# Neighbour sums in a graph network: one-hots compared with a row of numbers in PSUM and written tile by tile

## The chip, the cores and the metric

The kernel runs on one core of a Trainium2 chip, in one launch. Its time is the device time of that launch in microseconds (us); three runs are shown, with their median. A core has TensorE (PE, matrix products, with a separate row PEld for the loading of weights), VectorE (DVE), ScalarE (ACT), GpSimd (POOL) and SyncE (SP). SBUF is the working memory of 128 partitions, PSUM the smaller memory of eight banks into which TensorE writes.

## The reference

A graph of 12500 nodes with 32 features and 200000 edges, sorted by their target node, passes through four layers. The change touches the first only, a graph convolution that is applied three times:

```python
def _gcn_conv(x, src, dst, norm, W, b, n_nodes):
    h = x @ W
    msg = h[src] * norm[:, None]
    out = jax.ops.segment_sum(msg, dst, num_segments=n_nodes)
    return out + b
h = jax.nn.relu(_gcn_conv(x, src, dst, norm, W1, b1, n))
h = jax.nn.relu(_gcn_conv(h, src, dst, norm, W2, b2, n))
h = jax.nn.relu(_gcn_conv(h, src, dst, norm, W3, b3, n))
```

`norm` is a factor by node on each side, so what has to be summed for a node are rows of a table at `src`. After this layer come an attention over the same edges, a relational layer with edge types and a tensor product with edge attributes. Each gathers rows by edge and sums them by target node too.

## The kernel before, in words

The program is a row of blocks, one after the other; a barrier of all engines stands between two blocks. After the edges are sorted and tables are made, the three neighbour sums follow (`first_sums`, `second_sums`, `third_sums`; their tiles are called `sum0g`, `sum1g`, `sum2g` in the profile), then attention (`pass`), relational layer (`rel`) and tensor product (`sh`).

A neighbour sum takes the 200000 edges in 98 groups (`NG`) of 16 tiles of 128 edges (`GT` = 16). The rows to be summed are kept in device memory as three 16-bit parts whose sum is the 32-bit value. Five queues work on it:

- GpSimd issues one indirect DMA per tile of 128 edges (`_gather_groups`, L1241): 98 times 16, so 1568 gathers per sum. They write into a ring with four slots, one group each. Before a group it waits until its slot is free (L1237 to L1241, the semaphore `released`).
- SyncE passes on that a group has landed and that a slot is free (`_pass_groups`, L1244 and on; L1252 is where its word "landed" goes out).
- ScalarE copies the landed rows out of the ring (`copy_rows`, L1309, L1310, L1306) in the first and third sum. In the second TensorE reads the ring itself.
- VectorE makes, for each pair of a group and a tile of 128 target nodes, sixteen one-hot matrices (`make_one_hot`, `_pair_one_hot`, L1232): entry (edge, node) is 1 where the edge's target is that node. There are 196 pairs (`NS`) per sum, about two per group. Four buffers hold one-hots, so they are made up to four pairs ahead.
- TensorE multiplies one-hots with rows, sixteen matmuls per pair into one of four PSUM banks (`multiply`, L1326; `multiply_landed`, L1340). VectorE folds the three parts (L1349) and adds them to the node's sum (L1352).

The order of VectorE's queue is written out in a loop: the one-hots of pair n, then the fold of pair n - 3, then for each four node tiles that are complete what turns the sums into the next layer's rows (in the first sum L1393, L1429 and L1434 to L1437; in the second L1517 and L1569 to L1577; in the third L1667 to L1695).

The one-hots are compared out of `columns`, a table in SBUF of 128 x 16 numbers of 16 bits, in which each number stands sixteen times in a row (written once, L809), with `group_rel`, the edge's target within the tile, also 16 bits. The result lies interleaved: for one node the sixteen tiles stand side by side, so TensorE's weights are read with a step of sixteen elements (`[:, :, g]`). `columns` also serves the counting of degrees (L868, L874).

The later layers make their one-hots otherwise (`_one_hot`, L627): the numbers 0 to 127 stand once, as 32-bit values, in a PSUM bank called `numbers` (`numbers_in_psum`, L969 to L972), and the result is written tile by tile, as 32-bit values.

Of the kernel before, what the change touches and what calls it, by code (L numbers as in the profile page):

```python
# [19 lines left out]
F32 = mybir.dt.float32  # L20
BF16 = mybir.dt.bfloat16
I32 = mybir.dt.int32
U32 = mybir.dt.uint32
ALU = mybir.AluOpType
# [4 lines left out]
P = 128  # L29
# [24 lines left out]
BANK = 512  # L54
# [4 lines left out]
GT = 16  # L59
# [909 lines left out]
def numbers_in_psum(nc, ctx, k):  # L969

    k["numbers"] = ctx.enter_context(nc.psum_tensor("numbers", [P, BANK], F32))
    on_vector(nc, "numbers", [lambda: nc.vector.tensor_copy(k["numbers"][:, 0:P], k["iota"][:])])  # L972
# [257 lines left out]
def _pair_one_hot(nc, k, out, n):  # L1230

    return nc.vector.tensor_tensor(out, k["columns"][:],  # L1232
                                   k["group_rel"][:, n * GT:(n + 1) * GT].unsqueeze(1).to_broadcast([P, P, GT]), ALU.is_equal)
# [24 lines left out]
class Gathered:  # L1258


    def __init__(self, nc, ctx, name, width, slots, held_rows, mark=0, lent=(), direct=False):
        sb, psum, sem = _scope(nc, ctx, name)
# [7 lines left out]
        if direct:  # L1270
            self.onehot = [a[:, h * P * GT:(h + 1) * P * GT].rearrange("p (v g) -> p v g", g=GT) for a in spare for h in range(2)]
        else:
            self.rows += [a[:, 0:GT * self.held].rearrange("p (g f) -> p g f", g=GT) for a in spare]
        self.onehot += [sb(f"onehot{h}", [P, P, GT], BF16)[:] for h in range(len(self.onehot), 4)]
# [44 lines left out]
    def multiply(self, pe, m):  # L1319

        if m >= 4:
            pe.wait_ge(self.folded, 2 * (m - 4) + 1)
        pe.wait_ge(self.made, m + 1)
        pe.wait_ge(self.copied, m + 1 + BASE)
        for g in range(GT):
            last = self.nc.tensor.matmul(self.totals[:, m % 4, 0:self.held], self.onehot[m % 4][:, :, g], self.rows[m % self.kept][:, g, :],  # L1326
                                         start=(g == 0), stop=(g == GT - 1))
        last.then_inc(self.multiplied, 1)

    def multiply_landed(self, pe, words, m):  # L1330
# [8 lines left out]
        for g in range(GT):  # L1339
            last = self.nc.tensor.matmul(self.totals[:, m % 4, 0:self.held], self.onehot[m % 4][:, :, g], rows[:, g, :],  # L1340
                                         start=(g == 0), stop=(g == GT - 1))
# [1645 lines left out]
def gnn_kernel(nc, io, out):  # L2987
    dram = scratch(nc)
    with ExitStack() as ctx:
        k = tables(nc, ctx)  # L2990
# [3 lines left out]
        with ExitStack() as grouped:  # L2994
# [7 lines left out]
            w = gcn_weights(nc, grouped, io)  # L3002
            with ExitStack() as spread:
# [15 lines left out]
        numbers_in_psum(nc, ctx, k)  # L3019
# [42 lines left out]
```

## Time and profile before

| what | us |
|---|---|
| median of three runs (16224.31 to 16244.80) | 16242.67 |
| profiled execution, span from its first to its last instruction | 13614.9 |
| first neighbour sum, 397 to 2437 us of the span | 2040 |
| second neighbour sum, 2437 to 4495 | 2058 |
| third neighbour sum, 4495 to 6554 | 2059 |

The profiled execution is known by its span only: the profile covers what lies between the first instruction and the last. The median is 2627.8 us longer than the span, and no instruction of the profile lies in that remainder. Busy times of an engine are sums over its instructions; "idle before" is the time that the engine stood still just ahead of them, with what ended it. "issue" means that the profile shows nothing that it waited for. TensorE's granted clock (PEclk) is a share of full speed, 2.4 GHz.

### The profile page before, as it was taken

To read this page: it belongs to the slowest core of one execution; us is meant where nothing else is said; L and a number is where in the kernel's file an instruction comes from. 1 tells how busy PE (TensorE), PEld (TensorE's weight loads), DVE (VectorE), ACT (ScalarE), POOL (GpSimd) and SP (SyncE) were. 2 spreads that over 40 slices of the span, in tenths; PEclk is the share of its full clock that TensorE was granted. 3 is DMA by queue.
4 is the path that set the end of the run, shared out by engine and by line. 5 is a ranking of instruction groups with operands and counts; after the bars stand their busy time and mean duration, and the time that the engine had idled before them with its cause. 6 is when DMAs were issued, how large, how long until landed. Compare 5 with 4: busy or idle time off the path is not lost. (4 is left out here: it accounts for less than half of the span.)

```text
span 13614.9 us, 111810 instructions
## 1 busy us (share of the span) xinstructions
PE 5376.6 (39%) x26510; PEld 3602.5 (26%) x26510; DVE 6036.2 (44%) x11115; ACT 1387.4 (10%) x2612; POOL 9561.6 (70%) x9876
## 2 busy tenths in 40 slices
PE   1111222333444111111122222248888887555556
PEld 1111111222222111111111111123333336444445
DVE  5211222111222111122357777779999993333332
ACT  1111111000000111111101111110000012000001
POOL 0677777777777777777577777637777766777774
PEclk9755555666666555555555555569999998777777
DMA  3111111222222111111333333324444443111112
GB/s 112 23 20 20 24 29 30 70 77 77 77 77 78 26 19 19 21 23 23 116 96 102 102 102 102 91 55 83 83 81 83 82 83 96 24 23 23 23 23 60
DMA packets 696198, 811.04 MB, mean 60 GB/s; under 512 B 319128, under 2 KB 467557, under 8 KB 689994
## 3 DMA queue, kind: packets, MB, share of 16 engines
q0 software_dynamic: 340624, 383.65, 15.8%
q1 hardware_dynamic: 226416, 294.04, 7.2%
q10 hardware_dynamic: 128330, 124.33, 3.2%
q8 instruction: 272, 4.46, 0.1%
q14 instruction: 556, 4.55, 0.1%
HBM read 657.74 MB, written 143.55 MB: 59 GB/s over the span
## 5 line engine op out<-in xcount | busy, mean ns | idle before, releaser
L1241 POOL DMA_INDIRECT sum0g_ring<-scratch_parts,k_group_src x1568 | 1536.7, 980 | 684.9 <-issue 477.5
L740 POOL DMA_INDIRECT pass_ring<-scratch_tab,k_src x1664 | 1635.7, 983 | 539.0 <-issue 506.9
L740 POOL DMA_INDIRECT rel_ring<-scratch_tab,k_src x1664 | 1583.6, 952 | 554.1 <-issue 494.1
L740 POOL DMA_INDIRECT sh_ring<-scratch_tab_next,k_src x1664 | 1570.0, 944 | 567.1 <-issue 506.8
L1241 POOL DMA_INDIRECT sum1g_ring<-scratch_parts,k_group_src x1568 | 1553.5, 991 | 502.9 <-issue 477.3
L1241 POOL DMA_INDIRECT sum2g_ring<-scratch_parts,k_group_src x1568 | 1552.0, 990 | 504.9 <-issue 477.5
L679 PE MATMUL rel_accumulator<-rel_message,rel_onehot 128*128 128x512 f32 x3328 | 1559.5, 612 | 390.7 <-DVE rel_message L2310 383.8
L679 PE MATMUL sh_accumulator<-sh_message,sh_onehot 128*128 128x248 f32 x3328 | 1203.7, 542 | 887.8 <-DVE sh_message L2744 883.6
L679 PEld LDWEIGHTS sh_accumulator<-sh_message,sh_onehot 128*128 128x128 f32 x3328 | 946.1, 291 | 1144.8 <-issue 968.1
L1326 PE MATMUL sum2g_totals<-sum2g_rows,sum2g_onehot 128*128 128x96 bf16 x3136 | 282.3, 280 | 1728.9 <-ACT sum2g_rows L1306 1715.5
L2310 DVE TENSOR_TENSOR rel_message<-numbers,rel_ring 128x2048 f32<-128x2048 f32 x416 | 953.3, 2291 | 14.3
L679 PEld LDWEIGHTS rel_accumulator<-rel_message,rel_onehot 128*128 128x128 f32 x3328 | 606.0, 192 | 1068.4 <-issue 1068.4
L2741 DVE TENSOR_TENSOR sh_message<-sh_factors,sh_ring 128x1024 f32<-128x1024 f32 x208 | 254.7, 1225 | 1335.1 <-DMA sh_ring<-scratch_tab_next,k_src 1335.1
L1349 DVE TENSOR_REDUCE sum1g_joined<-sum1g_totals 128x128 f32<-128x384 f32 x196 | 109.1, 557 | 1417.4 <-PE sum1g_totals L1340 1417.4
L1326 PEld LDWEIGHTS sum2g_totals<-sum2g_rows,sum2g_onehot 128*128 128x128 bf16 x3136 | 256.1, 161 | 1779.2 <-issue 1771.1
L1340 PE MATMUL sum1g_totals<-sum1g_ring,k_q 128*128 x1568 | 360.5, 398 | 669.0 <-SPq L1252 669.0
L2141 PE MATMUL pass_q_edge<-query_parts,pass_onehot_t 128*128 x1664 | 257.7, 259 | 919.2 <-DVE pass_product L1941 874.8
L1340 PE MATMUL sum1g_totals<-sum1g_ring,k_x_next 128*128 x1568 | 365.0, 402 | 622.7 <-SPq L1252 622.7
L1349 DVE TENSOR_REDUCE sum0g_joined<-sum0g_totals 128x33 f32<-128x99 f32 x196 | 50.5, 258 | 1223.5 <-PE sum0g_totals L1326 1223.5
L1326 PE MATMUL sum0g_totals<-sum0g_rows,sum0g_onehot 128*128 128x99 bf16 x1568 | 150.1, 286 | 883.3 <-ACT sum0g_rows L1310 881.1
L2156 PE MATMUL pass_accumulator<-pass_parts,pass_onehot 128*128 128x108 bf16 x1664 | 248.4, 308 | 611.4 <-DVE pass_parts L2050 611.4
L1349 DVE TENSOR_REDUCE sum2g_joined<-sum2g_totals 128x32 f32<-128x96 f32 x196 | 49.4, 252 | 917.9 <-PE sum2g_totals L1326 917.9
(429 smaller groups left out, 9910.7 us busy)
## 6 DMA issues: line engine op xcount, KB each, us to landing
rel_rel_rows<-scratch_rel_rows ACTq DMA_DIRECT2D x211, 256.0 KB
pass_rows<-scratch_rel_rows SPq DMA_DIRECT2D x208, 256.0 KB
scratch_kv<-pass_ring SPq DMA_DIRECT2D x208, 256.0 KB, 2.1
pass_kept<-scratch_kv SPq DMA_DIRECT2D x208, 256.0 KB, 3.3
rel_type_rows<-scratch_type_rows ACTq DMA_DIRECT2D x211, 172.0 KB
rel_ring<-scratch_tab,k_src POOLq DMA_INDIRECT x1672
pass_ring<-scratch_tab,k_src POOLq DMA_INDIRECT x1664
sh_ring<-scratch_tab_next,k_src POOLq DMA_INDIRECT x1664
```

Of the source, the lines that this page charges most:

```text
L679: self.nc.tensor.matmul(self.accumulator[:, bass.ds(self.banks[g], self.width)], onehot, rows, start=False, stop=True, skip_group_check=Tr ...
L740: nc.gpsimd.indirect_dma_start(out=ring[:, q, g, :], out_offset=None, in_=table, in_offset=bass.IndirectOffsetOnAxis(ap=k["src"][:, n * G ...
L1241: nc.gpsimd.indirect_dma_start(out=ring[:, n % slots, g, :], out_offset=None, in_=table, in_offset=bass.IndirectOffsetOnAxis(ap=k["group_s ...
L1326: last = self.nc.tensor.matmul(self.totals[:, m % 4, 0:self.held], self.onehot[m % 4][:, :, g], self.rows[m % self.kept][:, g, :], start=( ...
L1340: last = self.nc.tensor.matmul(self.totals[:, m % 4, 0:self.held], self.onehot[m % 4][:, :, g], rows[:, g, :], start=(g == 0), stop=(g == ...
L1349: self.nc.vector.tensor_reduce(self.joined[q][:], self.totals[:, m % 4, 0:self.held].rearrange("p (c f) -> p f c", c=3), axis=AX_X, op=ALU ...
L2141: last = nc.tensor.matmul(q_edge[:, b, at:at + W], onehot_t[i % 3][:, g * P:(g + 1) * P], q_nodes[:, bass.ds(tiles[g] * W - W, W)], start= ...
L2156: nc.tensor.matmul(accumulator[:, m % 2, bass.ds(slots[g], 3 * width)], onehot[m % 3][:, :, g], parts[m % 3][:, g, :], start=False, stop=T ...
L2310: nc.vector.tensor_tensor(message[m % 4][:].rearrange("p g (b f) -> p g b f", f=D), coef[:, m % 2, :, :].unsqueeze(3).to_broadcast([P, H, ...
L2741: nc.vector.tensor_tensor(m[:, :, 0:4 * D].rearrange("p g (c f) -> p g c f", f=D), f[:, :, 0:4].unsqueeze(3).to_broadcast([P, G, 4, D]), r ...
```

## The change

One function makes the pairs' one-hots. Its first operand was the 16-bit table in SBUF, interleaved; now it is a row of 128 numbers of 32 bits in a PSUM bank, repeated sixteen times by the access pattern. The second operand is the same row of 16-bit targets, but repeated along the node axis. The output has the same 2048 16-bit elements per partition in another order: tile by tile. TensorE's weights are then read as 128 adjacent elements. The row of numbers is written in a block of its own before the tables of the groups are made. The table `columns` is still written, for the degrees.

```diff
-def numbers_in_psum(nc, ctx, k):
+def numbers_in_psum(nc, ctx, k, name):
 
-    k["numbers"] = ctx.enter_context(nc.psum_tensor("numbers", [P, BANK], F32))
-    on_vector(nc, "numbers", [lambda: nc.vector.tensor_copy(k["numbers"][:, 0:P], k["iota"][:])])
+    k["numbers"] = ctx.enter_context(nc.psum_tensor(name, [P, BANK], F32))
+    on_vector(nc, name, [lambda: nc.vector.tensor_copy(k["numbers"][:, 0:P], k["iota"][:])])
...
 def _pair_one_hot(nc, k, out, n):
 
-    return nc.vector.tensor_tensor(out, k["columns"][:],
-                                   k["group_rel"][:, n * GT:(n + 1) * GT].unsqueeze(1).to_broadcast([P, P, GT]), ALU.is_equal)
+    return nc.vector.tensor_tensor(out, k["numbers"][:, 0:P].unsqueeze(1).to_broadcast([P, GT, P]),
+                                   k["group_rel"][:, n * GT:(n + 1) * GT].unsqueeze(2).to_broadcast([P, GT, P]), ALU.is_equal)
...
-            self.onehot = [a[:, h * P * GT:(h + 1) * P * GT].rearrange("p (v g) -> p v g", g=GT) for a in spare for h in range(2)]
+            self.onehot = [a[:, h * P * GT:(h + 1) * P * GT].rearrange("p (g v) -> p g v", g=GT) for a in spare for h in range(2)]
...
-        self.onehot += [sb(f"onehot{h}", [P, P, GT], BF16)[:] for h in range(len(self.onehot), 4)]
+        self.onehot += [sb(f"onehot{h}", [P, GT, P], BF16)[:] for h in range(len(self.onehot), 4)]
...
-            last = self.nc.tensor.matmul(self.totals[:, m % 4, 0:self.held], self.onehot[m % 4][:, :, g], self.rows[m % self.kept][:, g, :],
+            last = self.nc.tensor.matmul(self.totals[:, m % 4, 0:self.held], self.onehot[m % 4][:, g, :], self.rows[m % self.kept][:, g, :],
...
             w = gcn_weights(nc, grouped, io)
+            numbers_in_psum(nc, grouped, k, "group_numbers")
```

VectorE's queue gains one block, ahead of the one that makes the tables of the groups. The rows are of VectorE, with those of the changed kernel marked +; L972 writes the row of numbers, L1185 and L1184 are the branches around it, and `k_group_src` is the first table.

```order
 L1818 MEMSET gcn_qkv 128x384
 L1814 UNCONDITIONAL_BRANCH
+L1185 UNCONDITIONAL_BRANCH
+L972 COPY group_numbers<-k_iota 128x128
+L1184 UNCONDITIONAL_BRANCH
 L803 UNCONDITIONAL_BRANCH
 L806 MEMSET k_group_src 128x224
```

Nothing is moved past another instruction; three rows are put in.

In the neighbour sums the order on VectorE stays as it was, and only the compare's operand changes. These are the first rows of the first sum, of VectorE.

```order
 L1470 UNCONDITIONAL_BRANCH
-L1232 TENSOR_TENSOR sum0g_onehot<-k_columns,k_group_rel 128x2048 x4
+L1232 TENSOR_TENSOR sum0g_onehot<-group_numbers,k_group_rel 128x2048 x4
 L1219 TENSOR_LOAD k_group_words
 L1349 TENSOR_REDUCE sum0g_joined<-sum0g_totals 128x33
 L1352 ISA
 L1352 TENSOR_TENSOR gcn_sums<-gcn_sums,sum0g_joined 128x33
```

TensorE's rows are the same in both kernels.

## Rows read from the trace of the kernel before

**Rows 1.** Stretches of the three sums: busy us by engine, clock, DMA.

```profile
core 0: us, PE busy (x) PEld busy (x) DVE busy (x) ACT busy (x) POOL busy (x), PEclk, DMA share, GB/s
397.00:2437.00 2040.00, 392.76 (x3261) 295.63 (x3261) 383.75 (x741) 324.83 (x417) 1536.68 (x1569) 0.54 0.14 24
2437.00:4495.00 2058.00, 766.48 (x3480) 523.93 (x3480) 439.32 (x741) 31.45 (x50) 1553.50 (x1568) 0.67 0.29 77
4495.00:6554.00 2059.00, 323.19 (x3211) 270.95 (x3211) 384.03 (x899) 299.02 (x271) 1554.12 (x1570) 0.52 0.14 21
```

**Rows 2.** Groups of GpSimd: busy us, mean ns, idle before and its releasers.

```profile
L1241 POOL DMA_INDIRECT sum1g_ring<-scratch_parts,k_group_src x1568 | 1553.5, 991 | 502.9 <-issue 477.3 <-SPq L1248 25.6
L1241 POOL DMA_INDIRECT sum2g_ring<-scratch_parts,k_group_src x1568 | 1552.0, 990 | 504.9 <-issue 477.5 <-SPq L1248 27.4
L1241 POOL DMA_INDIRECT sum0g_ring<-scratch_parts,k_group_src x1568 | 1536.7, 980 | 684.9 <-issue 477.5 <-SPq L1248 207.3
```

**Rows 3.** Gathers by line: duration ns minimum/median/maximum, first and last start.

```profile
L1241 POOL DMA_INDIRECT sum0g_ring<-scratch_parts,k_group_src x1568: 940/944/1919, 397.2 to 2410.4; - x196
L1241 POOL DMA_INDIRECT sum1g_ring<-scratch_parts,k_group_src x1568: 942/946/1971, 2437.0 to 4466.8; - x196
L1241 POOL DMA_INDIRECT sum2g_ring<-scratch_parts,k_group_src x1568: 940/944/2003, 4495.2 to 6523.8; - x196
L740 POOL DMA_INDIRECT sh_ring<-scratch_tab_next,k_src x1664: 938/944/957, 11417.4 to 13493.3; - x185
```

**Rows 4.** Third sum, GpSimd: start us, duration us, idle before.

```profile
5504.20 0.94 POOL L1241 DMA_INDIRECT sum2g_ring<-scratch_parts,k_group_src  x1 [0.30 <-issue]
5505.45 1.95 POOL L1241 DMA_INDIRECT sum2g_ring<-scratch_parts,k_group_src  x1 [0.31 <-issue]
5507.71 1.33 POOL L1241 DMA_INDIRECT sum2g_ring<-scratch_parts,k_group_src  x1 [0.30 <-issue]
```

**Rows 5.** The same stretch, VectorE.

```profile
5505.36 1.22 DVE L1232 TENSOR_TENSOR sum2g_onehot<-k_columns,k_group_rel 128x2048 bf16<-128x2048 bf16 x1
5507.00 1.22 DVE L1232 TENSOR_TENSOR sum2g_onehot<-k_columns,k_group_rel 128x2048 bf16<-128x2048 bf16 x1
```

**Rows 6.** Later layers, both engines: compares and products out of PSUM, gathers beside them.

```profile
9998.86 2.29 DVE L2310 TENSOR_TENSOR rel_message<-numbers,rel_ring 128x2048 f32<-128x2048 f32 x1
9999.81 0.94 POOL L740 DMA_INDIRECT rel_ring<-scratch_tab,k_src  x1 [0.30 <-issue]
...
12499.31 1.22 DVE L627 TENSOR_TENSOR sh_onehot<-numbers,k_drel 128x1024 f32<-128x1024 f32 x1
12499.68 0.94 POOL L740 DMA_INDIRECT sh_ring<-scratch_tab_next,k_src  x1 [0.30 <-issue]
```

**Rows 7.** VectorE by line: duration ns minimum/median/maximum, first and last start.

```profile
L1232 DVE TENSOR_TENSOR sum0g_onehot<-k_columns,k_group_rel x196: 1209/1218/1227, 396.5 to 2378.1; 128x2048 bf16<-128x2048 bf16 x196
L2310 DVE TENSOR_TENSOR rel_message<-numbers,rel_ring x416: 2291/2291/2292, 9098.5 to 11218.0; 128x2048 f32<-128x2048 f32 x139
L627 DVE TENSOR_TENSOR sh_onehot<-numbers,k_drel x208: 1214/1215/1217, 11422.4 to 13488.0; 128x1024 f32<-128x1024 f32 x104
```

**Rows 8.** Other VectorE work of the sums, in the first and second: busy us, mean ns.

```profile
L1352 DVE TENSOR_TENSOR k_wide<-k_wide,sum1g_joined 128x128 f32 x196 | 57.4, 293 | 28.7 <-DVE sum1g_joined L1349 1.0
L1437 DVE TENSOR_TENSOR sum_parts<-sum_rest,sum_parts 128x512 bf16<-128x512 f32 x24 | 17.4, 724 | 0.8
```

**Rows 9.** First and last gather that ran longer while a compare was running.

```profile
397.17 1.47 POOL L1241 DMA_INDIRECT sum0g_ring<-scratch_parts,k_group_src  x1 [207.34 <-SPq L1248]
...
6510.93 1.33 POOL L1241 DMA_INDIRECT sum2g_ring<-scratch_parts,k_group_src  x1 [0.30 <-issue]
```

**Rows 10.** The block that writes `numbers` before attention, and what follows it.

```profile
6651.64 0.29 DVE L972 COPY numbers<-k_iota 128x128 f32<-128x128 f32 x1 [11.86 <-PEq L104]
...
6652.86 1.89 DVE L2239 CAST query_parts<-k_q 128x3328 bf16<-128x3328 f32 x1 [0.93 <-PEq L104]
```

**Rows 11.** Weights of TensorE: interleaved in the sums, adjacent in attention.

```profile
L1326 PEld LDWEIGHTS sum0g_totals<-sum0g_rows,sum0g_onehot x1568: 142/163/186, 421.7 to 2416.1; 128*128 128x128 bf16 x196
L2141 PEld LDWEIGHTS pass_q_edge<-query_parts,pass_onehot_t x1664: 102/105/106, 6676.5 to 8789.2; 128*128 128x128 bf16 x185
```

More of the change, by code:

```diff
@@ L1339, in multiply_landed @@
         for g in range(GT):
-            last = self.nc.tensor.matmul(self.totals[:, m % 4, 0:self.held], self.onehot[m % 4][:, :, g], rows[:, g, :],
+            last = self.nc.tensor.matmul(self.totals[:, m % 4, 0:self.held], self.onehot[m % 4][:, g, :], rows[:, g, :],
                                          start=(g == 0), stop=(g == GT - 1))
@@ L3018, in gnn_kernel @@
         late_weights(nc, ctx, io, k)
-        numbers_in_psum(nc, ctx, k)
+        numbers_in_psum(nc, ctx, k, "numbers")
         attention(nc, io, k, dram, k["q"])
```

## The prediction

> **What bounds the kernel now.** I read the stretches of the three sums first. In each, GpSimd is busy for about 1540 to 1554 us of 2040 to 2059, and no other engine for more than 767 [rows 1]. GpSimd's groups then say what its idle time is: of some 500 us all but 25 to 27 is "issue", 0.305 us before each of 1567 gathers; the rest (207.3 in the first sum) is the one wait before a sum's first gather [rows 2]. So inside a sum GpSimd never waits for a free slot. A sum lasts 1568 x (gather + 0.305 us), plus a tail after the last gather (2437 - 2411.4, some 26 us) that the change leaves. The third view is the spread of the gathers: the median is 944 or 946 ns, but the maximum 1919 to 2003, while in the tensor product 1664 gathers all lie within 938 to 957 [rows 3]. Something lengthens single gathers in the sums.
>
> The timeline shows what. The gather of 5505.45 starts 0.09 us behind a one-hot compare and takes 1.95 us; the compare ends at 5506.58, the gather 0.82 us later. The next compare ends at 5508.22 and the gather that started under it at 5509.04, again 0.82 us later [rows 4, 5]. An undisturbed gather has that 0.82 us left when it is 0.12 us old. So a gather that starts while a compare runs stops 0.12 us after its start until the compare is done. I went through all rows of the three sums in this way: of 201.4 us above 0.944 us a gather, 200.0 lie on 518 gathers that a compare of L1232 was running over; [rows 9] are the first and the last of them.
>
> **The change part by part.**
>
> *What goes.* Excess of the gathers over their median: first sum 1536.7 - 1568 x 0.944 = 56.5 us, second 1553.5 - 1568 x 0.946 = 70.2, third 1552.0 - 1568 x 0.944 = 71.8 [rows 2, 3]; together 198.5, of which 99.3% under compares (200.0 of 201.4): 197 us. It goes if the new compare leaves GpSimd alone. The nearest rows are instructions of the new form, one input from PSUM and one from SBUF. The product L2310 runs 2.29 us from 9998.86, the gather that starts inside it at 9999.81 takes 0.94; the compare L627, whose operands are those of the new compare but for the 16 bits, runs from 12499.31 and the gather at 12499.68 takes 0.94 [rows 6]. All 208 compares of the tensor product lie beside gathers of at most 957 ns [rows 3, 7]. What no row has is this form with a 16-bit second input and 16-bit output. The bounds for this term are 0 (it holds GpSimd as before; worse is a rival) and -198.5; I take -197, since the nearest rows show no trace of a hold.
>
> *A rule that speaks against it.* The trace shows GpSimd's indirect gathers held by a VectorE instruction with two SBUF inputs [rows 4, 5]. The Trainium skill (SBUF — State Buffer, Who interferes with whom) says that such an instruction contends with a GpSimd instruction that reads SBUF, not with one that only writes, and infers that descriptor generation, needing the write side, is not stalled by a tensor_tensor. By that inference no gather would be held by the compare and this term would be 0; the rows disagree, and they decide. The same section says that an instruction with at most one SBUF input, outside the modes that use two ports, does not contend; with that [rows 6] agree.
>
> *What the compare costs.* Today 2048 elements take 1.218 us, two elements per cycle. With 32-bit numbers from PSUM, 1024 elements take 1.215 us and a product over 2048 takes 2.291 us [rows 7]. I take 2.29 us, 1.07 more, for 588 compares: 629 us of VectorE time. Bounds: 1.22 (nothing lost, if the 16-bit side kept its pace) and 2.29. It lies beside GpSimd's gathers. VectorE is the busiest in the second sum with 439.3 us of 2058 [rows 1]; with 196 x 1.07 = 210 more it is 649, under a third. Behind a longer compare stand the fold of the next pair, then L1352 and the closing work of four node tiles; TensorE waits for them, ScalarE and the slot's release for TensorE. With two compares per group that is 2.1 us later at most, and the ring has four slots of 16 x 1.25 = 20 us each. Cost: 0. Its cover would be gone only if VectorE's work per group (439.3/98 = 4.5 us now, 649/98 = 6.6 then) came near 20 us; uncovered it would cost the whole 629. At the end of a sum no compare stands between the last folds, as they are made ahead. At its start four compares take 9.2 us rather than 4.9, while the first group is gathered for 20 us.
>
> *Weights.* Interleaved they load in 163 ns, adjacent ones in attention in 105 [rows 11]. TensorE is no bound in the sums, so 0; in the last pairs of three sums some 1 us might be won. I leave it at 0.
>
> *The new block.* One copy of 0.29 us and the barrier to the next block, 0.93 us, stand in the open: 1.2 us; the idle time ahead of the copy, 11.86 us, is mostly another block's DMAs [rows 10]. Bounds 1.2 and 12, taken 2: only a barrier is added.
>
> *What is late next.* Other VectorE instructions read SBUF twice too and stay: L1352 (0.29 us in the second sum), L1437 (0.72) and their like [rows 8]. Before the change they held almost nothing (1.4 us in all with everything that isn't a compare), because they follow a group's landing at a fixed distance and mostly start just behind a gather. A compare that is 1.07 us longer shifts them. With a gather every 1.25 us and random phase, an instruction of d us holds (d - 0.12)²/(2 x 1.25): 0.012 us at 0.29, 0.14 at 0.72. For 196 of L1352 in the second sum, about 24 x (L1435, L1437 and two shorter casts) in the first, L1517 in the second and some 20 short ones per four tiles in the third that is about 19 us. Bounds 0 and 19 at random phase; I take 5, since the first fold of each group keeps its phase.
>
> Sum: -197 + 2 + 5 + 0 = -190 us, so the span goes from 13614.9 to about 13425. The remaining 2627.8 us between span and median has no instruction in it and I take it as fixed: 16242.67 - 190 = 16053 us, 1.2% less.
>
> **The rivals.**
>
> *A, slower: the new compare holds the gathers too.* The place is the start of each gather that falls into a compare, now 2.29 us long. For it: the second input is still SBUF, and 16 bits wide, which no row of the later layers has. Against it: [rows 6] and the 938 to 957 ns of [rows 3]. Price: a compare longer than the 1.25 us between gathers catches one every time and holds it 2.29 - 0.12 - 0.62 = 1.54 us on average, 588 x 1.54 = 905 us, against 198 now: +707. Today's phases give 0.34 us a compare where random ones give (1.22 - 0.12)²/2.5 = 0.48; scaled so, +445. That is 16690 to 16950, say 16820. It decides as soon as the hold is there at all.
>
> *B, no change: the gathers are longer for another reason* that merely comes at the time of a compare, such as the ScalarE and TensorE burst when a group lands. For it: that burst has the same rhythm. Against it: the end of each long gather lies 0.82 us behind the end of a compare, to the hundredth. Time: 16242.67 + 2 = 16245. The skill's inference above would come out here.
>
> *C, the gain is partly given back in phase.* If the shifted folds and closing instructions came to start just before a gather in most groups, L1352 would cost 0.17 us in 196 pairs of the second sum (33 us) and three instructions of about 0.72 us per four tiles some 0.6 us each, 24 times (43 us), and the third sum's short ones some 20 more: about 95 us, 16148.
>
> *D, slower: VectorE's longer queue frees slots late.* As above: only at 20 us of work per group, with 629 us as its price less 197, 16675. At a third of that load I see no way to it.
>
> *E, more than forecast:* the 2627.8 us may be no fixed piece but a stretch of the whole run (16242.67/13614.9 = 1.193). Then 190 us of span are 227 of time: 16016.
>
> **How the numbers follow.** Chances: forecast 0.82, A 0.03, B 0.03, C 0.06, D 0.01, E 0.05. The forecast's own range takes the bounds of its terms: from -197 + 1 to -197 + 12 + 19, so 16047 to 16077, widened by the spread of the runs shown (18 us below the median, 2 above) to 16025 to 16085. To leave out no more than 2 in 10, also for an own error in the fixed remainder, the range takes in E and goes half-way to C: 16010 to 16105. A measurement of this kernel can tell 0.2%, 32 us, from no change. Faster by more: forecast, C, E, 0.93. Within: B, and a little of C, 0.03. Slower: A and D, 0.04.
>
> **What would show it.** Right, if in the profile of the changed kernel the gathers L1241 have a mean of about 945 to 950 ns in all three sums and a maximum near 1000 but for a few; the compares take 2.28 to 2.29 us; each sum is shorter by 57, 70 and 72 us less a few; GpSimd's idle time is still 477 us of "issue" per sum; a block of some 2 us stands before the tables of the groups. Wrong, if gathers of 2 us and more are still there (A), if the mean stays at 980 to 991 (B), if L1352 or L1437 now lie under long gathers (C), or if GpSimd waits for SyncE inside a sum (D).

## The result, and the profile after

The changed kernel takes 16319.44 us (median of 4 runs, 16317.73 to 16325.45), the kernel before 16243.74 in the same comparison (16224.31 to 16257.26). The ratio is 1.0045, with an interval of 1.0031 to 1.0059: 76 us slower, where 190 us less was forecast.

The first view is that of line L1241, the gathers, in the changed kernel; the columns are those of [rows 3], and below them stands what ended GpSimd's idle time.

```profile
L1241 POOL DMA_INDIRECT sum0g_ring<-scratch_parts,k_group_src x1568: 938/944/1092, 399.7 to 2690.6; - x196
L1241 POOL DMA_INDIRECT sum1g_ring<-scratch_parts,k_group_src x1568: 940/946/1467, 2744.1 to 4985.3; - x196
L1241 POOL DMA_INDIRECT sum2g_ring<-scratch_parts,k_group_src x1568: 938/944/1030, 5020.2 to 7314.9; - x196
...
  issue: 1398.6, 4581
  SPq L1255: 981.9, 120
  SPq L1248: 293.8, 3
```

The median is 944 to 946 ns as before, but the maxima of 1919, 1971 and 2003 in [rows 3] are 1092, 1467 and 1030 now: the long gathers are gone. New is the wait for SyncE's L1255, the release of a slot in the ring: 981.9 us in 120 places. [rows 2] have none of it. The same by group, with the columns of [rows 2]:

```profile
L1241 POOL DMA_INDIRECT sum1g_ring<-scratch_parts,k_group_src x1568 | 1489.6, 950 | 805.1 <-issue 461.7 <-SPq L1255 290.8 <-SPq L1248 52.6
L1241 POOL DMA_INDIRECT sum0g_ring<-scratch_parts,k_group_src x1568 | 1479.9, 944 | 1019.2 <-issue 470.3 <-SPq L1255 341.6 <-SPq L1248 207.3
L1241 POOL DMA_INDIRECT sum2g_ring<-scratch_parts,k_group_src x1568 | 1479.6, 944 | 850.0 <-issue 466.6 <-SPq L1255 349.5 <-SPq L1248 33.9
```

The means fell from 980, 991 and 990 to 944, 950 and 944 ns, busy time from 4642.2 to 4449.1 us: −193, where the forecast's terms for the gathers were −197 and +5. Idle time rose by more. The compare, in the columns of [rows 7]:

```profile
L1232 DVE TENSOR_TENSOR sum0g_onehot<-group_numbers,k_group_rel x196: 2277/2283/2291, 399.0 to 2724.9; 128x2048 bf16<-128x2048 f32 x196
```

2283 ns, where the forecast took 2290. The stretches of the three sums, with the columns of [rows 1]:

```profile
core 0: us, PE busy (x) PEld busy (x) DVE busy (x) ACT busy (x) POOL busy (x), PEclk, DMA share, GB/s
400.00:2744.00 2344.00, 483.46 (x3261) 295.07 (x3261) 590.09 (x741) 329.78 (x417) 1479.62 (x1568) 0.69 0.13 21
2744.00:5020.00 2276.00, 904.46 (x3480) 420.53 (x3480) 639.54 (x741) 31.38 (x50) 1489.63 (x1568) 0.64 0.26 69
5020.00:7345.00 2325.00, 398.36 (x3209) 268.53 (x3209) 586.34 (x887) 299.06 (x270) 1479.63 (x1568) 0.51 0.12 18
```

A sum lasts 2276 to 2344 us, in [rows 1] 2040 to 2059. That comparison misleads, though. The page after has a span of 16315.9 us in an execution of 16317.73: the span is the time. The page before has a span of 13614.9 beside a median of 16242.67. Its record is of another execution, one that ran 2.6 ms quicker than those timed. Every row ahead of the prediction comes from it.

### The profile page after: what moved, and what is told of

Same layout as the page of the kernel before. It is cut to its first block and busy times, and to the rows that moved or that the text cites. A ratio compares the mean times of both kernels' runs of the same rounds, so it can differ in the third digit from the quotient of the medians.

```text
span 16315.9 us, 111836 instructions
## 1 busy us (share of the span) xinstructions
PE 5773.1 (35%) x26510; PEld 3391.3 (21%) x26510; DVE 6647.9 (41%) x11116; ACT 1393.6 (9%) x2612; POOL 9388.7 (58%) x9876
## 5 line engine op out<-in xcount | busy, mean ns | idle before, releaser
L679 PE MATMUL rel_accumulator<-rel_message,rel_onehot 128*128 128x512 f32 x3328 | 1759.6, 678 | 1192.7 <-DVE rel_message L2310 989.0
L1241 POOL DMA_INDIRECT sum0g_ring<-scratch_parts,k_group_src x1568 | 1479.9, 944 | 1019.2 <-issue 470.3
L1241 POOL DMA_INDIRECT sum2g_ring<-scratch_parts,k_group_src x1568 | 1479.6, 944 | 850.0 <-issue 466.6
L1241 POOL DMA_INDIRECT sum1g_ring<-scratch_parts,k_group_src x1568 | 1489.6, 950 | 805.1 <-issue 461.7
L679 PE MATMUL sh_accumulator<-sh_message,sh_onehot 128*128 128x248 f32 x3328 | 1070.2, 450 | 1421.9 <-issue 1368.9
L679 PEld LDWEIGHTS sh_accumulator<-sh_message,sh_onehot 128*128 128x128 f32 x3328 | 758.1, 230 | 1733.5 <-issue 1663.4
L679 PEld LDWEIGHTS rel_accumulator<-rel_message,rel_onehot 128*128 128x128 f32 x3328 | 683.5, 216 | 1980.8 <-issue 1980.8
L1326 PE MATMUL sum2g_totals<-sum2g_rows,sum2g_onehot 128*128 128x96 bf16 x3136 | 355.9, 266 | 1906.8 <-issue 1210.5
L627 DVE TENSOR_TENSOR sh_onehot<-numbers,k_drel 128x1024 f32<-128x1024 f32 x208 | 253.8, 1220 | 1716.7 <-DMA rl_current<-scratch_tab,k_last_index 1083.5
L627 DVE TENSOR_TENSOR rel_onehot<-numbers,k_drel 128x512 f32<-128x512 f32 x419 | 287.8, 687 | 1008.5 <-DMA k_ends<-scratch_ends 514.6
L1340 PE MATMUL sum1g_totals<-sum1g_ring,k_x_next 128*128 x1568 | 432.7, 413 | 644.1 <-SPq L1252 344.5
```

What stands on the lines that cost most here:

```text
L627: return nc.vector.tensor_tensor(out[:], k["numbers"][:, 0:P].unsqueeze(1).to_broadcast([P, n, P]), k["drel"][:, bass.ds(first, n)].unsque ...
L679: self.nc.tensor.matmul(self.accumulator[:, bass.ds(self.banks[g], self.width)], onehot, rows, start=False, stop=True, skip_group_check=Tr ...
L1241: nc.gpsimd.indirect_dma_start(out=ring[:, n % slots, g, :], out_offset=None, in_=table, in_offset=bass.IndirectOffsetOnAxis(ap=k["group_s ...
```

## Experiments

The runs below were made on three chips. On two of them the kernel before took 13.62 to 13.63 ms (medians), on the third 16.11 to 16.13 ms, with at most 0.6% between the runs of a chip. Times are compared only between runs of one chip that were made together; profiles of the two kinds of chip are set side by side to see what differs.

The texts put down before each run name these theories:

- Theory 1: the gathers are held by a VectorE instruction with two SBUF inputs, and the change ends that. In the executions of 16 ms TensorE is at times issued slowly, in both kernels; the ring of gathered rows fills, and then the loss comes from the longer compare, because VectorE sets the pace at which the backlog goes.
- Theory 2: the change itself brings TensorE's slow stretches, by the reads of PSUM or (2b, the theory by the layout) by the one-hots' new order in SBUF.
- Theory 3: gathers that nothing holds make TensorE's slow stretches longer.
- Another rival: the gathers are long for a reason other than the hold.

**Both kernels again, unchanged, where the kernel before takes 13626.78 us (7 runs).**

> The kernel before, unchanged, profiled once more. Theory 1 (the execution on which the prediction rests was of another kind than the timed ones: in those TensorE is at times issued one matmul per 1.4 to 2.8 us, the ring fills, and what VectorE needs per pair then sets how fast the backlog goes): the span is 16.2 ms, TensorE's matmuls of the sums show such stretches, GpSimd waits for slots (SPq L1255) some 500 to 900 us in the three sums, and the gathers still have their excess of some 200 us. Theory 2 (the stretches are brought by the change, by the reads of PSUM or the adjacent weights): the span is 13.6 ms, or 16.2 with stretches only outside the sums, and no wait for slots.

> The changed kernel, unchanged, profiled once more, to see what varies between executions of one kernel. Theory 1: 16.32 ms again, waits for slots of 900 to 1050 us in the sums, stretches of slow issue at other places in the program. Theory 2: the same places to within a few us.

Measured: 13604.83 and 13442.94 us, one run each; the second is 184 us below the median of before. GpSimd's groups, first of the kernel before, then of the changed one:

```profile
L1241 POOL DMA_INDIRECT sum1g_ring<-scratch_parts,k_group_src x1568 | 1554.8, 992 | 502.8 <-issue 477.3 <-SPq L1248 25.6
L1241 POOL DMA_INDIRECT sum2g_ring<-scratch_parts,k_group_src x1568 | 1539.1, 982 | 505.7 <-issue 477.5 <-SPq L1248 28.1
L1241 POOL DMA_INDIRECT sum0g_ring<-scratch_parts,k_group_src x1568 | 1535.9, 980 | 685.1 <-issue 477.6 <-SPq L1248 207.6
```

```profile
L1241 POOL DMA_INDIRECT sum1g_ring<-scratch_parts,k_group_src x1568 | 1490.8, 951 | 503.4 <-issue 477.8 <-SPq L1248 25.6
L1241 POOL DMA_INDIRECT sum2g_ring<-scratch_parts,k_group_src x1568 | 1484.2, 947 | 505.8 <-issue 477.8 <-SPq L1248 28.0
L1241 POOL DMA_INDIRECT sum0g_ring<-scratch_parts,k_group_src x1568 | 1483.5, 946 | 685.7 <-issue 477.8 <-SPq L1248 207.9
```

Here the forecast holds: gathers 4629.8 to 4458.5 us (−171, with a median that was 3 ns higher in this record, 947 for 944, which is 14 us), "issue" 477 per sum as in [rows 2], and no wait for L1255 in either. So the change brings what was said on such a chip, and something else turns it round on the other kind.

**The changed kernel's compare with its numbers from SBUF, as 32-bit numbers.** It changes one operand's memory and nothing else:

```diff
-    return nc.vector.tensor_tensor(out, k["numbers"][:, 0:P].unsqueeze(1).to_broadcast([P, GT, P]),
+    return nc.vector.tensor_tensor(out, k["iota"][:].unsqueeze(1).to_broadcast([P, GT, P]),
```

> The changed kernel, but the row of 32-bit numbers is read from SBUF (the iota table), not from PSUM: two SBUF inputs, the same 2048 elements at one per cycle, written tile by tile. The compare takes 2.29 us in every theory. Theory 1: gathers are held again, now under a longer compare, 445 to 707 us of excess over the changed kernel; where GpSimd waits for slots this is hidden, so the time is 16320 + 250 to 600 = 16570 to 16920. Theory 2 (it is the reading of PSUM that costs): no slower than before, under 16300.

> sbuf32 again (32-bit numbers from SBUF, compare of 2.28 us that holds gathers). Where the kernel before takes 13.6 ms it cost 684 us. Where it takes 16.1 to 16.2 ms theory 1 expects less, since waits for slots hide part of the holds: 1.02 to 1.04 of before, 300 to 650 us more.

Measured 14310.57 us (ratio to before 1.0499, 1.0481 to 1.0516) and 14314.79 (1.0504, 1.0486 to 1.0521). The compares last 2284 ns, as with PSUM, and its gathers are these:

```profile
L1241 POOL DMA_INDIRECT sum0g_ring<-scratch_parts,k_group_src x1568: 941/947/2734, 402.8 to 2621.6; - x196
L1241 POOL DMA_INDIRECT sum1g_ring<-scratch_parts,k_group_src x1568: 942/949/2994, 2647.8 to 4935.0; - x196
L1241 POOL DMA_INDIRECT sum2g_ring<-scratch_parts,k_group_src x1568: 943/947/3067, 4965.5 to 7213.1; - x196
```

Median 947 to 949, maximum up to 3067 ns, means 1111, 1155 and 1129. The time is 868 us above the changed kernel of the same chip, more than the 445 to 707 expected; the gathers' excess over their median is 865 us, all of it in the open, since nothing waits for a slot on this chip. The hold is the two SBUF inputs' doing, and the rival "another reason" has fallen.

**The same PSUM bank with a 16-bit table.** The kernel before, its one-hots interleaved as ever, but with each number eight times as 16 bits in one PSUM bank, and each of these rows of eight used twice:

```diff
-    return nc.vector.tensor_tensor(out, k["columns"][:],
-                                   k["group_rel"][:, n * GT:(n + 1) * GT].unsqueeze(1).to_broadcast([P, P, GT]), ALU.is_equal)
+    return nc.vector.tensor_tensor(out.rearrange("p v (a t) -> p v a t", t=8),
+                                   k["short"].unsqueeze(2).to_broadcast([P, P, GT // 8, 8]),
+                                   k["group_rel"][:, n * GT:(n + 1) * GT].rearrange("p (a t) -> p a t", t=8).unsqueeze(1)
+                                   .to_broadcast([P, P, GT // 8, 8]), ALU.is_equal)
```

> The kernel before, but the interleaved 16-bit table lies in one PSUM bank, each number eight times, and is used twice per node; output and weights interleaved as before. One input from PSUM, both 16-bit with adjacent elements innermost. If the compare keeps its two elements per cycle it takes 1.2 us and holds no gather. Theory 1: the gathers lose their excess and the queue of VectorE stays short: 100 to 200 us faster than before, 16050 to 16140. If a PSUM input costs the pace (2.29 us): like the changed kernel, 16320. Theory 2: slower than before although the compare is short, 16300 or more.

> table8 again (16-bit table in PSUM, compare of 1.2 us, no held gathers, interleaved weights), for a chip on which the kernel before takes 16.1 to 16.2 ms. There, theory 1 (after each fetch of 16 KB of instructions TensorE runs some 60 instructions slowly, and the backlog then goes at VectorE's pace, 2.7 us per pair in the changed kernel against 1.65 to 1.8 before): faster than before by 0 to 200 us and faster than the changed kernel by 80 to 250. Theory 3 (undisturbed gathers make TensorE's slow stretches longer): slower than before by 50 to 120 us, as the changed kernel. On a chip where the kernel before takes 13.6 ms: 0.986 of it, both.

> table8 once more, hoping for a slow chip. There, theory 1: 0 to 200 us faster than before and at least 80 us faster than filler_second. Theory 3: as much slower than before as the changed kernel (50 to 120 us). On a fast chip 13442 us as twice.

Measured 13441.85 (0.9864, 0.9848 to 0.988), 13442.61 (0.9864) and 13422.41 us (0.9852). Line L1232 of its profile:

```profile
L1232 DVE TENSOR_TENSOR sum0g_onehot<-short_columns,k_group_rel x196: 1209/1217/1226, 397.4 to 2326.9; 128x2048 bf16<-128x2048 bf16 x196
```

It keeps the 1217 ns of the old compare and leaves the gathers alone (means 946, 951 and 947 ns). It gains what the changed kernel gains without the longer compare. On this chip 1.07 us more per compare are worth nothing, as the forecast had it.

**The changed kernel with the old order of the one-hots**, and **the 16-bit table with a copy of 768 elements per pair as filler on VectorE**:

```diff
-    return nc.vector.tensor_tensor(out, k["numbers"][:, 0:P].unsqueeze(1).to_broadcast([P, GT, P]),
-                                   k["group_rel"][:, n * GT:(n + 1) * GT].unsqueeze(2).to_broadcast([P, GT, P]), ALU.is_equal)
+    return nc.vector.tensor_tensor(out, k["numbers"][:, 0:P].unsqueeze(2).to_broadcast([P, P, GT]),
+                                   k["group_rel"][:, n * GT:(n + 1) * GT].unsqueeze(1).to_broadcast([P, P, GT]), ALU.is_equal)
...
+        self.nc.vector.tensor_copy(self.filled[:], k["short_words"][:, 0:24].unsqueeze(1).to_broadcast([P, 32, 24]))
```

> The changed kernel with the old interleaved layout: numbers of 32 bits in PSUM, but one-hots written with the sixteen tiles side by side and weights read with a step of sixteen. The compare should take 2.28 us as in the changed kernel. Before at 16.1 to 16.2 ms: theory 1 and 3, 1.003 to 1.007 of before, as the changed kernel; theory 2b (adjacent weights bring the loss): not slower than before. Before at 13.6 ms: 0.986 of it in all.

> table8 with one more VectorE instruction per pair, a copy of 768 elements from PSUM into a tile that nothing reads, some 0.95 us, ahead of the compare. VectorE then needs about as much per pair as in the changed kernel and holds no gather; weights stay interleaved. Before at 16.1 to 16.2 ms: theory 1, as the changed kernel, 1.003 to 1.007 of before. Theory 3 or a theory by the layout of the weights: as table8_second within 30 us. Before at 13.6 ms: as table8, within 10 us.

> table8_filler once more, hoping for a slow chip. There, theory 1: 1.003 to 1.007 of before, as the changed kernel. Theory 3 or layout: as table8_third within 30 us. On a fast chip 13442 us as before.

Measured 13445.46 (0.9866, 0.985 to 0.9883), 13441.99 (0.9865) and 13421.41 us (0.985). All four versions without the hold (the changed kernel, this one, the 16-bit table and that with the filler) are equal on either chip of 13.6 ms; the question of layout or pace can only be put where TensorE falls behind. None of the last three was run undelayed on a chip of 16 ms.

**Both kernels again, unchanged, where the kernel before takes 16132.37 us (11 runs).**

> The kernel before, unchanged, for its profile. If this chip is one on which it takes 16.2 ms: theory 1 (slow issue of TensorE in both kernels; a longer compare then lies behind it) expects the stretches and the waits for slots in this record too, in the three sums some 600 to 900 us of waits against 982 of the changed kernel, and later layers as in the changed kernel within 30 us. If it takes 13.6 ms: no waits for slots, as in the first record.

> The changed kernel, unchanged, timed beside the one before. Where the kernel before takes 13.6 ms: 0.986 to 0.987 of it, as the first call had in single runs. Where it takes 16.2 ms: 1.003 to 1.006. Theory 1 expects the sign to go with the time of the kernel before, a rival (chance differences between executions) expects both signs in either.

Measured: 16131.33 us, and 16219.2 us for the changed kernel (8 runs; ratio 1.0053, 1.0036 to 1.0069). GpSimd's groups, before and changed:

```profile
L1241 POOL DMA_INDIRECT sum1g_ring<-scratch_parts,k_group_src x1568 | 1567.2, 999 | 704.8 <-issue 468.5 <-SPq L1255 196.8 <-SPq L1248 39.5
L1241 POOL DMA_INDIRECT sum2g_ring<-scratch_parts,k_group_src x1568 | 1564.8, 998 | 715.5 <-issue 478.4 <-SPq L1255 202.4 <-SPq L1248 34.7
L1241 POOL DMA_INDIRECT sum0g_ring<-scratch_parts,k_group_src x1568 | 1553.2, 991 | 900.3 <-issue 477.5 <-SPq L1255 216.0 <-SPq L1248 206.8
```

```profile
L1241 POOL DMA_INDIRECT sum1g_ring<-scratch_parts,k_group_src x1568 | 1488.2, 949 | 792.1 <-issue 462.8 <-SPq L1255 276.8 <-SPq L1248 52.5
L1241 POOL DMA_INDIRECT sum0g_ring<-scratch_parts,k_group_src x1568 | 1480.1, 944 | 1011.7 <-issue 478.7 <-SPq L1255 326.0 <-SPq L1248 207.1
L1241 POOL DMA_INDIRECT sum2g_ring<-scratch_parts,k_group_src x1568 | 1479.8, 944 | 844.7 <-issue 466.6 <-SPq L1255 335.8 <-SPq L1248 42.4
```

So the slow stretches and the slot waits are there without the change, 615.2 us of waits in the kernel before; the changed one has 938.6. The sign of the change goes with the kind of chip. The balance over the three sums: gathers −237, L1255 +323, L1248 +21, "issue" −16. From the first gather to the first one of the next stage it is 6939.2 us against 7027.8, +89, and the medians differ by 87. What makes the slots late is TensorE. One of its groups, busy us and mean ns, then idle us by releaser, in the kernel before on the 13.6 ms chip and then on this one:

```profile
L1326 PE MATMUL sum2g_totals<-sum2g_rows,sum2g_onehot 128*128 128x96 bf16 x3136 | 282.7, 280 | 1715.9 <-ACT sum2g_rows L1306 1702.5 <-DVE sum2g_onehot L1232 13.4
```

```profile
L1326 PE MATMUL sum2g_totals<-sum2g_rows,sum2g_onehot 128*128 128x96 bf16 x3136 | 325.1, 265 | 1908.8 <-issue 1018.5 <-ACT sum2g_rows L1306 805.9 <-DVE sum2g_onehot L1232 82.2
```

1018.5 us of "issue", waits for nothing that the profile shows, stand where there was none. In the timeline (start us, duration us, idle before):

```profile
842.01 0.24 PE L1326 MATMUL sum0g_totals<-k_q,sum0g_onehot 128*128 128x99 bf16 x1 [2.56 <-issue]
844.82 0.24 PE L1326 MATMUL sum0g_totals<-k_q,sum0g_onehot 128*128 128x99 bf16 x1 [2.56 <-issue]
847.62 0.24 PE L1326 MATMUL sum0g_totals<-k_q,sum0g_onehot 128*128 128x99 bf16 x1 [2.56 <-issue]
```

One matmul of 0.24 us each 2.8 us, and the stretches that follow in this sum, with the columns of [rows 1]:

```profile
814.00:834.00 20.00, 1.70 (x7) 1.13 (x8) 1.59 (x3) 1.68 (x2) 15.12 (x17) 0.50 0.13 20
894.00:914.00 20.00, 1.71 (x7) 0.99 (x7) 1.59 (x3) 1.68 (x2) 11.53 (x13) 0.50 0.11 16
914.00:934.00 20.00, 9.04 (x94) 7.46 (x93) 7.78 (x16) 7.93 (x10) 5.26 (x5) 0.63 0.03 5
```

Seven matmuls and seven or eight weight loads in 20 us, from 814 to some 924, then 94 in 20 us. A 16 KB instruction fetch of queue q8 lies between 813 and 815; in the changed kernel one lies between 750 and 755 and its slow stretch begins at 754. The profile lists the same 272 packets of q8 in the records of 13.6 ms, where no such stretch follows. In the first sum, called sum 0 here, the time from the first to the last matmul of a pair adds up to 237 to 244 us in the record of 13.6 ms, and to 1343 here (41 pairs above 4 us; 1641 and 63 in the changed kernel). What on a chip makes it so stays open.

These figures show one thing more: TensorE's slow stretches are more frequent in the changed kernel. I counted the matmuls that start more than 1 us behind the one before them in the same pair: 928 in the three sums of the kernel before (2190 us in all), 1261 in the changed kernel (2735 us). In sum 0 both records have 27 fetches of q8; 20 or more such matmuls follow 11 of them before the change and 17 after it. So theory 2 is wrong in that the change doesn't bring the stretches, but whether their growth comes from VectorE's pace, from the layout or from the undisturbed gathers (theory 3) no undelayed run shows.

Behind such a stretch several groups wait, and all pairs go at the pace of the engine that does most per pair. VectorE in the kernel before, just after it:

```profile
925.89 1.22 DVE L1232 TENSOR_TENSOR sum0g_onehot<-k_columns,k_group_rel 128x2048 bf16<-128x2048 bf16 x1
927.03 0.25 DVE L1349 TENSOR_REDUCE sum0g_joined<-sum0g_totals 128x33 f32<-128x99 f32 x1
927.42 0.20 DVE L1352 TENSOR_TENSOR gcn_sums<-gcn_sums,sum0g_joined 128x33 f32 x1
927.53 1.24 DVE L1232 TENSOR_TENSOR sum0g_onehot<-k_columns,k_group_rel 128x2048 bf16<-128x2048 bf16 x1
...
929.20 1.22 DVE L1232 TENSOR_TENSOR sum0g_onehot<-k_columns,k_group_rel 128x2048 bf16<-128x2048 bf16 x1
```

A compare each 1.64 to 1.67 us: fold, L1352, compare, with no idle time. And in the changed kernel, VectorE and then TensorE:

```profile
741.57 2.28 DVE L1232 TENSOR_TENSOR sum0g_onehot<-group_numbers,k_group_rel 128x2048 bf16<-128x2048 f32 x1
743.77 0.25 DVE L1349 TENSOR_REDUCE sum0g_joined<-sum0g_totals 128x33 f32<-128x99 f32 x1
744.16 0.19 DVE L1352 TENSOR_TENSOR gcn_sums<-gcn_sums,sum0g_joined 128x33 f32 x1
744.27 2.28 DVE L1232 TENSOR_TENSOR sum0g_onehot<-group_numbers,k_group_rel 128x2048 bf16<-128x2048 f32 x1
...
746.98 2.28 DVE L1232 TENSOR_TENSOR sum0g_onehot<-group_numbers,k_group_rel 128x2048 bf16<-128x2048 f32 x1
```

```profile
743.95 1.49 PE L1326 MATMUL sum0g_totals<-k_x_next,sum0g_onehot 128*128 128x99 bf16 x16 [1.21 <-issue]
746.66 1.49 PE L1326 MATMUL sum0g_totals<-sum0g_rows,sum0g_onehot 128*128 128x99 bf16 x16 [1.21 <-issue]
749.36 1.49 PE L1326 MATMUL sum0g_totals<-sum0g_rows,sum0g_onehot 128*128 128x99 bf16 x16 [1.21 <-issue]
```

A compare each 2.70 us; TensorE does its 16 matmuls in 1.49 us and sits idle for 1.21. Each pair of such a backlog costs 1.06 us more, and the slot that GpSimd waits for comes free that much later.

The second sum is a check on this. Its products are of 384 columns, a matmul starts 163 ns behind the one before, and TensorE alone needs some 2.65 us a pair; so the longer compare moves the pace of a backlog from 2.65 to 3.1 us only. From the first to the last gather the first sum loses 38 us (2246.7 to 2284.8) and the third 37, while the second gains 5 (2232.5 to 2227.8). That fits the pace, but the slow starts counted above also grow least in the second sum (207 to 239, against 419 to 588 and 302 to 434), so it doesn't decide between pace and slow stretches.

**TensorE made late by repeated products.** Pairs 6 to 10 of every 16 have their products 18 times (9 times in the second sum), in either kernel, on the chip of 16.1 ms:

```diff
+def SLOW(m, times=18):
+    return times if m % 16 in (6, 7, 8, 9, 10) else 1
...
-        for g in range(GT):
+        for g in [g for again in range(SLOW(m)) for g in range(GT)]:
```

> The kernel before, but TensorE repeats the products of five of every sixteen pairs (18 times in the first and third sum, 9 times in the second; each repetition starts the sum anew, so the result is the same), which makes such a pair last some 24 to 28 us. Theory 1: GpSimd now waits for slots; the sums take 100 to 500 us longer than in the kernel before, and part of the 200 us of held gathers is hidden in these waits. Rival (a slow TensorE hides nothing): as much longer as slow_after is.

> The changed kernel with the same repetitions. Theory 1: the gain over slow_before is less than half of the 184 us seen without the repetitions, or a loss of up to 100 us, since gathers wait for slots and VectorE's longer compare stands between a pair's product and the next. Rival: the gain is the whole 184 us, within 20.

Measured 18924.57 (1.174, 1.1711 to 1.1768) and 18705.14 us (1.1605, 1.1576 to 1.1634): the changed kernel 219 us quicker, against theory 1. The repetitions cost the kernel before 2.8 ms, where 0.1 to 0.5 was expected. The experiment is confounded. In the long rows of products a matmul of the first sum starts every 63 ns (median) with interleaved weights and every 47 ns with adjacent ones (63 and 43 in the third); with some 32,600 additional matmuls in these two sums, 16 to 20 ns each are 520 to 650 us in the changed kernel's favour. As a whole it tells nothing of the compare. In the second sum a matmul starts every 163 ns in either layout; there the changed kernel takes 155 us more (3138.4 and 3293.5 us from the first to the last gather), though its gathers are 83 us shorter.

**TensorE made late by the same work in both.** 60 products of zeros, 512 columns each, ahead of two of every eight pairs; they have the same weights in both kernels:

```diff
+        for again in range(60 if m % 8 < 2 else 0):
+            self.nc.tensor.matmul(self.totals[:, m % 4, :], Gathered.k["ident"][:], Gathered.k["zeros"][:], start=True, stop=True)
```

> The kernel before, but TensorE runs 60 products of 512 columns of zeros ahead of the products of two of every eight pairs, in the bank that the pair then starts anew: a stall of some 60 us in all per eight pairs, the rhythm of the slow stretches seen in the 16 ms executions. On a chip where the kernel before takes 13.6 ms, theory 1: eight pairs take 60 us of stall and 8 x 1.65 at VectorE's pace, 74 us, less than the 82 us plus holds in which GpSimd gathers four groups: 0 to 150 us longer than the kernel before. On a slow chip: 17 ms or more.

> The changed kernel with the same stalls. Fast chip, theory 1: 60 us of stall and 8 x 2.7 at VectorE's pace, 82 us or a little more, so the gain of 184 us over cyc_before shrinks to under 120 or turns into a loss, depending on the exact length of the stalls. Theory 3 or one by layout (nothing of VectorE's pace): the whole 184 us, within 20.

Measured on a chip where the kernel before takes 13622.3: 16722.2 (1.2277, 1.2256 to 1.2297) and 16922.37 us (1.2422, 1.2402 to 1.2443). The 60 products took 51.7 us (they stand as 120 records), so a stall of two pairs took 103 us and not the 60 expected: TensorE became what bounds the sums, and the kernel before took 3.1 ms longer rather than at most 150 us. What follows a stall in the changed kernel's first sum is TensorE's side of the backlog:

```profile
1593.70 0.91 PE L1328 MATMUL sum0g_totals<-k_x_next,sum0g_onehot 128*128 128x99 bf16 x16
1594.45 0.90 PE L1328 MATMUL sum0g_totals<-sum0g_rows,sum0g_onehot 128*128 128x99 bf16 x16
1596.06 0.91 PE L1328 MATMUL sum0g_totals<-sum0g_rows,sum0g_onehot 128*128 128x99 bf16 x16 [0.71 <-issue]
1598.77 0.91 PE L1328 MATMUL sum0g_totals<-k_q,sum0g_onehot 128*128 128x99 bf16 x16 [1.80 <-issue]
1601.47 1.49 PE L1328 MATMUL sum0g_totals<-k_x_next,sum0g_onehot 128*128 128x99 bf16 x16 [1.80 <-issue]
```

The pairs whose one-hots were ready follow 0.75 us apart; then they come each 2.70 us, the compare's pace. The changed kernel, 184 us quicker without stalls, is 200 us slower with them. The first sum's group of either:

```profile
L1241 POOL DMA_INDIRECT sum0g_ring<-scratch_parts,k_group_src x1568 | 1531.1, 976 | 1488.3 <-SPq L1255 813.9 <-issue 467.4 <-SPq L1248 207.0
```

```profile
L1241 POOL DMA_INDIRECT sum0g_ring<-scratch_parts,k_group_src x1568 | 1479.8, 944 | 1663.2 <-SPq L1255 991.3 <-issue 464.8 <-SPq L1248 207.2
```

Gathers −51.3 us, slot waits +177.4. Stalls alone turn the sign, on a chip that has none of its own, so more frequent slow stretches aren't needed for a loss. By sum the change costs 124 us in the first, −22 in the second and 83 in the third (first to last gather). These runs don't tell pace from layout.

**The 16-bit table with those stalls, without and with the filler.** The layout is the same in both; only VectorE's pace differs, 1.64 and 2.50 us a pair:

> table8 (compare of 1.2 us, no held gathers, old layout) with the stalls of cyc_before. Theory 1 (VectorE's pace behind a stall): as cyc_before or a little faster, 16650 to 16730 on a fast chip. Theory by undisturbed gathers: as cyc_after, 16900.

> table8_filler (0.95 us more of VectorE work per pair, else as table8) with the same stalls. Theory 1: 150 to 220 us slower than cyc_table8, as cyc_after is than cyc_before. Theory by the layout: as cyc_table8 within 30 us.

Measured where the kernel before takes 16113.65: 21479.36 (1.3328, 1.3305 to 1.335) and 21619.88 us (1.341, 1.3388 to 1.3432), 140.5 us for 0.86 us of pace. Theory 1 said 150 to 220, layout at most 30: it is the pace, and the size is a little under what was expected. TensorE's own slow stretches are the same in both (833 and 804 matmuls more than 1 us behind the one before), so the slower pace did not multiply them, and the loss is again in the first and third sum (79 and 34 us, 2 in the second). The filler that costs nothing in an undisturbed run costs 140 us once TensorE is late. How much the layout or theory 3 adds undelayed these runs don't say.

## Why the prediction was wrong

- *What goes, −197.* Right. The gathers lost 193 us of busy time against [rows 2], and 171 between two records of one chip; the mechanism of [rows 4, 5] is shown by the run with both inputs in SBUF. It was right, too, to conclude from the nearest rows, [rows 6], that the new form holds no gather. Rival A's price for a longer compare that does hold them, 905 us of holds and +707, was near what the run with both inputs in SBUF measured, 865 us and +684.
- *What is late next, 5.* Right: 1568 times the medians of the changed kernel (944, 946 and 944 ns) are 4443.7 us, so 5.4 us of excess remain of 198.5. With *the new block, 2*, and *weights, 0*, the sum was −190; on a chip of 13.6 ms −184 was measured, in one run against the median of seven. (Adjacent weights loaded in 143 ns there, not in the 105 of [rows 11], which changes nothing in the sum.)
- *"The remaining 2627.8 us between span and median has no instruction in it and I take it as fixed."* This is the step that failed first. It was no piece of the timed executions that lies outside the span: in the other records span and time are less than 3 us apart. It was time inside the span that the record shown had not spent, in the sums behind TensorE's slow stretches, of which that record had none. Of the 2526 us between the two unchanged records, 696 lie in the sums (6243.1 and 6939.2 us), the rest in later stages. A gap of 19% between a record's span and the median said that the rows were of another kind of execution; the forecast took it as a fixed remainder, and rival E only scaled it.
- *"Cost: 0" for the compare, hidden beside the gathers.* It rested on [rows 1, 2], where GpSimd never waits for a slot. In the timed executions it waits 615 us before and 939 after, so 1.07 us more per compare stood in the open wherever VectorE set the pace of a backlog; with TensorE late in both, 0.86 us more per pair cost 140 us.
- *Rival D* named the right mechanism, "VectorE's longer queue frees slots late", and gave it 1 in 100, as "only at 20 us of work per group". That is a condition on the mean. What decides is the pace within a backlog: fold, L1352 and compare, 1.64 us a pair against 2.70 in the first and third sum, which matters as soon as TensorE has been late.
- Its own test said so: *"if GpSimd waits for SyncE inside a sum (D)"*. It does. "Issue" was 461.7 to 470.3 us per sum, near the 477 foretold. Rivals A, B and C fell with the maxima and means of the gathers.

What stays open: how the +323 us of slot waits divide. The sums are then partly bound by TensorE's stretches, so some of the 237 us won in gathers is lost there without any doing of the compare, and some by the slower pace; a part may also lie with the slow stretches themselves, which are more frequent in the changed kernel (1261 slow starts for 928), and for that layout and theory 3 stand untested. That the pace costs time once TensorE is late is shown; that it makes up the whole loss of the timed executions is not. They were not separated in undelayed runs on a chip of 16 ms. The 16-bit table should keep the one without paying the other, but undelayed it was only run on chips of 13.6 ms, where it equals the changed kernel; that it beats both kernels elsewhere is not shown.

## What to carry to other kernels

Before a row is trusted, compare the record's span with the timed median; if they differ by more than the 3 us at most of the other records here, the rows are of an execution with other bounds, and each "hidden" must be asked again for the slower one. Work is hidden in a ring of buffers only while nobody is behind: price an addition both by the mean load and by the pace at which a backlog is worked off. Where an operand's place holds another engine, try first to change the place and keep the width: the 16-bit table in PSUM ended the hold at 1217 ns, the 32-bit one at 2283.

## What the runs showed of the hardware

- A compare of 2048 elements with a 16-bit table in PSUM and a 16-bit SBUF input takes 1217 ns, as with both in SBUF; with a 32-bit PSUM input 2283 ns.
- With two SBUF inputs a compare of 2284 ns made the 1568 gathers of a sum 257 to 322 us longer than 1568 times their median; with one input from PSUM, of 16 or 32 bits, the excess was at most 6.3 us.
- On one chip TensorE was issued one instruction per 0.7 to 1.4 us for about 110 us behind many of its instruction fetches (in the first sum 11 of 27 in the kernel before, 17 of 27 in the changed one), on two others never; the same program took 16.1 and 13.6 ms.
- Dense matmuls of the first sum, 128x128 weights and 99 columns, started every 63 ns with interleaved weights and every 47 ns with adjacent ones (medians). At a granted clock of 1.0 (2.4 GHz) these were 62 and 47 ns, at 0.5 (1.2 GHz) 82 in both.
